# Edge tiles beside the first 7 of 8 groups in three joined stages of a graph network

## The chip, the cores and the metric

The kernel runs on one core of a Trainium2 chip. The metric is the device time of one execution in microseconds (us). Three runs of the kernel before took 3811.76, 3812.99 and 3815.6 us; the median is 3812.99.

## The reference

The input `x` has 10000 nodes of 512 features, and there are 5000 edges, sorted by target. Four graph layers follow each other, each as `x = layernorm(x + layer(x))`: a GIN layer, a SAGE layer with a batch norm, a layer of two graph attentions (GAT) and a product, and a GCN layer with a batch norm. Only the last two matter here:

```python
def gat_conv(x, src, dst, W, a_src, a_dst, bias):
    h = (x @ W).reshape(n, H, C)                       # H = 4, C = 256
    al_s = jnp.einsum('nhc,hc->nh', h, a_src)
    al_d = jnp.einsum('nhc,hc->nh', h, a_dst)
    e = jax.nn.leaky_relu(al_s[src] + al_d[dst], NEG_SLOPE)
    w = jnp.exp(e - segment_max(e, dst)[dst])
    alpha = w / segment_sum(w, dst)[dst]
    out = segment_sum(h[src] * alpha[:, :, None], dst)
    return out.reshape(n, H * C) + bias
...
h = relu(gat_conv(x, src, dst, W1, a_src1, a_dst1, b1))    # W1: 512 x 1024
h = relu(gat_conv(h, src, dst, W2, a_src2, a_dst2, b2))    # W2: 1024 x 1024
h @ Wfc + bfc                                              # Wfc: 1024 x 512
...
msgs = norm[:, None] * (x @ W.T)[row]                      # the GCN layer
out = segment_sum(msgs, col)
```

src and dst hold the edges and one loop from each node to itself.

## The kernel before, in words

The nodes are put in an order of the kernel's own and padded to 10240 rows, which makes 20 groups of 4 subtiles of 128 rows (S = 4). Nodes that are no edge's target stand first. The first 8 groups (`d.early`, E = 8) hold such nodes alone: their rows depend on no edge. The 5000 edges fill T = 40 tiles of 128. A float32 product is made of three float16 products (`split_product`, lines 350 to 352: low times high, high times low, high times high).

The program is a list of stages. At a stage's end all five engines meet, and none starts the next stage before. Inside a stage each engine has its own list, written out by hand, and they are held together by semaphores alone.

Three stages are joined: they work on the 8 edge-free groups and, beside them, on the edges' tiles, whose sums the stage behind needs for the other 12 groups.

- The middle stage, `gat_middle_early_stage`: the product with W2 for 8 groups. Each of 32 subtiles has three thirds of 344 columns, 24 matmuls each, so there are 96 slots, each one product. The edges' tiles are those of the first attention.
- The rows stage, `rows_product_early_stage`: the product with Wfc, 24 matmuls of 512 columns for each of 32 subtiles, so 32 slots. In a slot TensorE first turns two chunks of the next group (L3102), then makes the product. VectorE adds the product to the rows `x` (the residual, L3046, in float32), takes their moments (L1847, L1850) and, after slot 1 of the next group, applies the norm in `finish` (L1867). GpSimd makes the low halves (L3022), the norm's power (L1856, L1859) and starts the gathers. SyncE loads the rows to come (`load_rows`), `x` (`load_x`, L2987) and stores the results (`store`, L2992). The edges' tiles are those of the second attention.
- The GCN stage, `gcn_early_stage`: the product with the GCN's W, 12 matmuls for each of 32 pairs of group and quarter, so again 32 slots. Its edges' tiles are plain weighted sums (`RowEdges`).

`AttentionEdges` has T + 5 = 45 steps. Step e below 40 is tile e: TensorE multiplies the gathered rows by the mixing matrix `a_lhs` (L1700, eight passes), then sums the weights of the tile after (L1687) and turns the scores of the one after that (L1679). VectorE's step e makes the matrix of tile e + 1 (L1509 to L1521) and the maxima of tile e + 2. ScalarE copies the sums out (L1665), SyncE stores them with the first and the last row apart (L1450 to L1452). Steps 40 to 44 are the join of targets that lie in two tiles: VectorE waits until every tile is stored and spreads the last rows (step 40, L1546, L1547), TensorE turns them (step 41, L1714), VectorE and ScalarE weigh them (step 42), TensorE turns the weights (step 43, L1718) and VectorE copies them (L1586), TensorE sums the rows (step 44, L1723) and VectorE adds them (L1593), and SyncE stores (L1461). `RowEdges` has 41 steps: 40 tiles (L1827, two passes; copied out at L1811) and one join step, in which TensorE itself waits for all stores and sums the last rows (L1819); VectorE's part of it (`vector_end`, L1789, L1791) stands after its whole loop, and SyncE's store after that.

`shared_out` says which steps go behind which product. In all three stages each engine runs, for slot n, its part of the product and then its part of every step in `steps[n]`:

```python
steps = shared_out(edges.steps(), E * S)
...
for s in range(S):
    if g + 1 < E:
        turn(g + 1, (2 * s, 2 * s + 1))
    ...
    for e in steps[g * S + s]:
        edges.tensor_step(pe, e)
```

SyncE stores a tile one slot later than the others work on it (`waiting`).

Of the kernel before, what the change touches and what calls it, by code (L numbers as in the profile page):

```python
# [18 lines left out]
S = 4  # L19
# [12 lines left out]
THIRDS = 3  # L32
# [1794 lines left out]
        pe.matmul(self.total[t % 2][:], self.lhs[t % self.L], self.rows[w], start=True, stop=True).then_inc(self.summed.sem, 1)  # L1827


def shared_out(steps, slots):  # L1830

    return [range(n * steps // slots, (n + 1) * steps // slots) for n in range(slots)]
class Norm:


# [734 lines left out]
def gat_middle_early_stage(kn):  # L2570
# [4 lines left out]
    E = d.early  # L2575
    N = E * S
# [29 lines left out]
    wide_done = take("wide_done", THIRDS * N)  # L2606
    wide_stored = pair("wide_stored", 16 * 2 * E)
    edges = AttentionEdges(kn, mem, dram["h1"])
    steps = shared_out(edges.steps(), THIRDS * N)

    def sync(sp):
        def load_rows(j):
# [330 lines left out]
def rows_product_early_stage(kn):  # L2943
# [4 lines left out]
    E = d.early  # L2948
# [22 lines left out]
    rows_out = take("rows_out0", S * E)  # L2971
    stored = pair("stored", 16 * (E // 2))
    edges = AttentionEdges(kn, mem, dram["h2"])
    steps = shared_out(edges.steps(), E * S)

    def sync(sp):
        def load_rows(g):
# [406 lines left out]
def gcn_early_stage(kn, held):  # L3384
# [4 lines left out]
    E = d.early  # L3389
# [13 lines left out]
    seen = take("h_seen", 4 * E)  # L3403
    room = [held.rows[g][m] for g in range(E, E + 3) for m in range(4)]
    edges = RowEdges(kn, room, dram["x3"], (kn.src_by[:, :, 0], kn.src_dinv_neg), kn.dst_dinv, kn.rim_dinv)
    steps = shared_out(edges.steps(), 4 * E)

    def sync(sp):
        def load(g):
# [324 lines left out]
def graph_layers_kernel(nc, nodes, edges, io):  # L3734
# [16 lines left out]
    with ExitStack() as ctx:  # L3751
        kn = Kernel(nc, ctx, d, dram)
        tables = Tables(kn)
        with ExitStack() as mem:
            setup = setup_stage(kn, mem, tables)
            weights = plain_weights(kn, mem, list(range(W_SAGE_L + 1)), 3)
            sums = edge_sum_stage(kn, mem, dram["x"], None, None, None, tables)
            kn.add({
                "sync": in_turn(weights["sync"], setup["sync"], sums["sync"], setup["sync_late"]),
                "gpsimd": in_turn(setup["gpsimd"], sums["gpsimd"]),  # L3760
                "scalar": in_turn(setup["scalar"], weights["scalar"], sums["scalar"]),
                "vector": in_turn(setup["vector"], weights["vector"], sums["vector"]),
                "tensor": in_turn(setup["tensor"], sums["tensor"])})
        kn.add(gin_stage(kn))
        with ExitStack() as mem:
            kn.add(edge_product_stage(kn, mem))
        kn.add(sage_stage(kn))
        kn.add(norm_coefficients_stage(kn, V_SAGE_G, V_SAGE_BETA, 1.0 / UNSCALE))
        kn.add(batch_norm_stage(kn, "sage"))
        kn.add(gat_middle_early_stage(kn))  # L3770
        kn.add(gat_middle_stage(kn))
        kn.add(rows_product_early_stage(kn))
        kn.add(gat_stage(kn, 2))
        with ExitStack() as mem:
            held = Held(kn, mem)
            kn.add(gcn_early_stage(kn, held))
            kn.add(gcn_stage(kn, held))
            kn.add(norm_coefficients_stage(kn, V_GCN_G, V_GCN_BETA))
            kn.add(output_stage(kn, held))
        kn.run()  # L3780
# [60 lines left out]
```

How the kernel before makes its waits and increments, by code:

```python
        def program(eng, which):  # L310
            self.sig.raise_all(eng, ENGINES.index(which))
            eng.drain().then_inc(meet, 1)
            eng.wait_ge(meet, 5)
            for n, stage in enumerate(stages):
                if which in stage:
                    stage[which](eng)
                eng.drain().then_inc(meet, 1)
                eng.wait_ge(meet, 5 * (n + 2))
# [207 lines left out]
    def sync(sp):  # L526
        sp.dma_start(pairs[:], dram["edges"]).then_inc(pairs_in.sem, 16)
        sp.dma_start(dst_row, dram["dst"].partition_broadcast(P)).then_inc(dst_in.sem, 16)
        sp.dma_start(kn.vec[:], dram["vectors"]).then_inc(small_in.sem, 16)
        sp.dma_start(kn.gin_b2[:], dram["gin_b2"].partition_broadcast(P)).then_inc(small_in.sem, 16)
        sp.dma_start(kn.fc_b[:], dram["fc_b"].partition_broadcast(P)).then_inc(small_in.sem, 16)
        sp.wait_ge(blank_ready.sem, blank_ready.at(1))
        sp.dma_start(dram["sum"][d.none:d.none + 1, :], blank[0:1, 0:D]).then_inc(tables.zeroed.sem, 16)
        sp.dma_start(dram["sum_gat"][d.none:d.none + 1, 0:HC], blank[0:1, 0:HC]).then_inc(tables.zeroed.sem, 16)
        sp.dma_start(dram["sum_gat"][d.none:d.none + 1, HC:], kn.ones[0:1, 0:HEADS]).then_inc(tables.zeroed.sem, 16)
# [1 line left out]
    def sync_late(sp):  # L538
        sp.wait_ge(degrees.sem, degrees.at(2))
        sp.wait_ge(place_steps.sig.sem, place_steps.sig.at(9))
        sp.dma_start(dram["by_node"].rearrange("(p r) c -> p (r c)", p=P), kn.by_node[:].rearrange("p r c -> p (r c)"))\
```

## Time and profile before

| | us |
|---|---|
| three runs | 3811.76, 3812.99, 3815.6 |
| the profiled execution, its own time | 3817.86 |
| its span, from the first to the last instruction | 3816.0 |
| TensorE busy | 3332.8 (87% of the span) |
| VectorE busy | 1998.9 (52%) |
| ScalarE busy | 1430.8 (37%) |
| GpSimd busy | 1638.7 (43%) |
| products of the middle stage | 1645 to 2079 |
| products of the rows stage | 2650 to 2976 |
| products of the GCN stage | 3337 to 3467 |

Engines are called PE (TensorE matmul), PEld (its weight loads), DVE (VectorE), ACT (ScalarE), POOL (GpSimd) and SP (SyncE). A busy share is an average over stages with different limits, so each stage is read by itself. In a timeline a row gives the start and the length in us, and in brackets the idle time before it and what ended that. Matmuls overlap: a matmul's start to the next one's start is what it costs.

### The profile page before, as it was taken

Reading aid. Unit: us, or ns where it says so; the run is one execution under the profiler, and the core shown is the slowest. Engines: PE = TensorE matmul, PEld = TensorE weight load, DVE = VectorE, ACT = ScalarE, POOL = GpSimd, SP = SyncE. Lnnn points to the kernel's source line nnn. Section 1 sums busy time; section 2 is a strip of 40 time slices with the busy share of each in tenths; the row PEclk is TensorE's granted clock in tenths of the full one; section 3 lists DMA queues with packets and bytes.
Section 4 is the critical chain, followed back from the end, with each engine's and each line's share of the span. In section 5 each row is a group of like instructions: output and inputs, shape, how many; then the busy total and the mean of one; then the engine's idle time right before and its main releaser. Section 6 shows DMA issues by size and latency. Waiting matters only on the chain. (4 is left out here: it accounts for less than half of the span.)

```text
span 3816.0 us, 54506 instructions
## 1 busy us (share of the span) xinstructions
PE 3332.8 (87%) x18968; PEld 2029.2 (53%) x18968; DVE 1998.9 (52%) x3718; ACT 1430.8 (37%) x2551; POOL 1638.7 (43%) x1419
## 2 busy tenths in 40 slices
PE   4669998989988999979998899998989599897953
PEld 3224443445645766657775566665655355453543
DVE  7347776754545444244442643402766488433676
ACT  1323332443324444333332333323544244253366
POOL 3347775323547666322111432312544466322346
PEclk7789999989989999989999999998999799998975
DMA  2667774655659989698884989844775577366466
GB/s 82 202 174 197 201 196 122 222 163 182 213 193 252 284 270 274 198 233 224 223 217 139 259 210 207 199 109 157 223 240 183 214 258 259 138 214 172 144 216 225
DMA packets 601425, 771.73 MB, mean 202 GB/s; under 512 B 382934, under 2 KB 383190, under 8 KB 599200
## 3 DMA queue, kind: packets, MB, share of 16 engines
q1 hardware_dynamic: 525344, 535.62, 47.5%
q0 software_dynamic: 75904, 233.90, 21.4%
q8 instruction: 93, 1.52, 0.2%
q14 instruction: 84, 0.69, 0.1%
HBM read 420.55 MB, written 263.75 MB: 179 GB/s over the span
## 5 line engine op out<-in xcount | busy, mean ns | idle before, releaser
L351 PE MATMUL bank<-w_lo,t_r_hi 128*128 128x344 f16 (+1 forms) x2560 | 839.1, 328 | 0.0
L352 PE MATMUL bank<-w_hi,t_r_hi 128*128 128x344 f16 (+1 forms) x2560 | 838.8, 328 | 0.0
L350 PE MATMUL bank<-w_hi,w_lo 128*128 128x344 f16 (+1 forms) x2240 | 717.0, 320 | 47.2 <-DMA w_lo<-g_row_lo 31.3
L351 PE MATMUL bank<-w_lo,w_hi 128*128 128x344 f16 (+1 forms) x1280 | 420.3, 328 | 0.0
L352 PE MATMUL bank<-w_hi 128*128 128x344 f16 (+1 forms) x1280 | 420.0, 328 | 0.0
L350 PE MATMUL bank<-w_hi 128*128 128x344 f16 (+1 forms) x1216 | 396.8, 326 | 22.9 <-DMA w_hi<-t_row_lo 19.4
L352 PEld LDWEIGHTS bank<-w_hi,t_r_hi 128*128 128x128 f16 x2560 | 251.4, 98 | 169.6 <-issue 1.7
L351 PEld LDWEIGHTS bank<-w_lo,t_r_hi 128*128 128x128 f16 x2560 | 251.4, 98 | 160.9 <-issue 1.3
L350 PEld LDWEIGHTS bank<-w_hi,w_lo 128*128 128x128 f16 x2240 | 219.9, 98 | 178.9 <-issue 42.8
L1438 POOL DMA_INDIRECT a_own<-h,edge_tables x80 | 82.2, 1028 | 533.8 <-PE bank L1700 388.0
L350 PE MATMUL bank<-l_z_hi,w_lo 128*128 128x512 f16 x640 | 245.1, 383 | 1.4 <-DVE l_z_lo L3562 1.4
L2875 DVE SCALAR_TENSOR_TENSOR t_z<-w_lo,t_z 128x256 f32<-128x256 f32 x192 | 139.5, 784 | 203.2 <-DMA w_lo<-h 200.7
L351 PE MATMUL bank<-l_z_lo,w_hi 128*128 128x512 f16 x640 | 245.1, 383 | 0.0
L352 PE MATMUL bank<-l_z_hi,w_hi 128*128 128x512 f16 x640 | 244.9, 383 | 0.0
L2849 POOL TENSOR_TENSOR t_row_lo<-t_r,t_row_hi 128x1024 f16<-128x1024 f32 x48 | 105.7, 2203 | 281.9 <-ACT t_row_hi L2896 281.8
L2515 ACT ACTIVATE b_wide<-bank 128x344 f32<-128x344 f32 x240 | 109.0, 456 | 252.6 <-PE bank L352 251.3
L1700 PE MATMUL bank<-a_rows,a_lhs 128*128 128x256 f32 x640 | 158.0, 391 | 23.9 <-DVE a_lhs L1521 23.9
L350 PEld LDWEIGHTS bank<-w_hi 128*128 128x128 f16 x1216 | 119.8, 99 | 96.9 <-issue 21.4
L352 PEld LDWEIGHTS bank<-w_hi 128*128 128x128 f16 x1280 | 125.9, 98 | 85.1 <-issue 0.8
L351 PEld LDWEIGHTS bank<-w_lo,w_hi 128*128 128x128 f16 x1280 | 125.8, 98 | 84.0 <-issue 0.7
L1878 POOL DMA_INDIRECT t_z<-sum_gat,slot_i x96 | 99.9, 1040 | 116.9 <-SPq L317 91.2
L1700 PEld LDWEIGHTS bank<-a_rows,a_lhs 128*128 128x128 f32 x640 | 121.8, 195 | 47.7 <-DVE a_lhs L1521 28.8
(413 smaller groups left out, 6889.3 us busy)
## 6 DMA issues: line engine op xcount, KB each, us to landing
w_lo<-h SPq DMA_DIRECT2D x154, 512.0 KB, 6.3
h<-b_wide SPq DMA_DIRECT2D x80, 516.0 KB, 3.4
h<-w_hi SPq DMA_DIRECT2D x80, 516.0 KB, 2.9
sum_gat<-a_out SPq DMA_DIRECT2D x80, 514.0 KB
sum<-e_out SPq DMA_DIRECT2D x80, 256.0 KB
g_x<-in_x SPq DMA_DIRECT2D x20, 1024.0 KB, 5.4
x<-g_y SPq DMA_DIRECT2D x20, 1024.0 KB, 5.0
h<-l_h SPq DMA_DIRECT2D x20, 1024.0 KB, 6.1
```

Of the source, the lines that this page charges most:

```text
L350: pe.matmul(out, s_lo, m_hi, start=(k == 0), stop=False)
L351: pe.matmul(out, s_hi, m_lo, start=False, stop=False)
L352: mm = pe.matmul(out, s_hi, m_hi, start=False, stop=last)
L1438: pool.indirect_dma_start(self.own[w][:], None, self.logits_dram, bass.IndirectOffsetOnAxis(ap=kn.dst_logits_i[:, t:t + 1], axis=0), bound ...
L1700: ins = pe.matmul(self.total[h // 2][:, (h % 2) * C:(h % 2 + 1) * C], self.lhs[:, h, :], self.rows[w][:, LOGITS + h * C:LOGITS + (h + 1) * ...
L1878: pool.indirect_dma_start(out, None, sums, bass.IndirectOffsetOnAxis(ap=kn.slot_i[:, g * S + s:g * S + s + 1], axis=0), bounds_check=kn.d. ...
L2515: act.activation(wide[s][:, n * THIRD:(n + 1) * THIRD], mm[n], ACT.Copy, scale=UNSCALE)\
L2849: nc.gpsimd.tensor_tensor(row_lo[:, s, :], r_f[s % 2][:], row_hi[:, s, :], ALU.subtract)\
L2875: ins = v.scalar_tensor_tensor(out=z[u][:, s, cols], in0=hrow[:, s, cols], scalar=z[u][:, s, HC + h:HC + h + 1], in1=z[u][:, s, cols], op0 ...
```

## The change

`shared_out` takes a number of slots at the end that get no step. The steps are spread over the slots before them. In the middle stage 12 of 96 slots are left free, in the two others 4 of 32: in each, those of the last group. Every engine's list follows, since all of them read `steps`.

```diff
-def shared_out(steps, slots):
-
-    return [range(n * steps // slots, (n + 1) * steps // slots) for n in range(slots)]
+def shared_out(steps, slots, free):
+
+    used = slots - free
+    return [range(n * steps // used, (n + 1) * steps // used) if n < used else range(0) for n in range(slots)]
...
-    steps = shared_out(edges.steps(), THIRDS * N)
+    steps = shared_out(edges.steps(), THIRDS * N, THIRDS * S)
...
-    steps = shared_out(edges.steps(), E * S)
+    steps = shared_out(edges.steps(), E * S, S)
...
-    steps = shared_out(edges.steps(), 4 * E)
+    steps = shared_out(edges.steps(), 4 * E, 4)
```

## Rows read from the trace of the kernel before

**Rows 1.** Busy time in stretches: middle stage, its first group, rows stage, GCN stage.

```profile
core 0: us, PE busy (x) PEld busy (x) DVE busy (x) ACT busy (x) POOL busy (x), PEclk, DMA share, GB/s
1652.00:2083.00 431.00, 426.02 (x2837) 308.27 (x2835) 180.93 (x496) 146.43 (x316) 72.87 (x72) 1.00 0.79 203
1645.00:1699.00 54.00, 51.10 (x328) 36.44 (x329) 22.23 (x59) 17.68 (x37) 8.02 (x8) 0.97 1.08 231
2656.00:2977.00 321.00, 293.87 (x1523) 186.99 (x1521) 215.00 (x560) 148.67 (x302) 145.04 (x140) 0.97 0.65 203
3340.00:3467.00 127.00, 127.00 (x564) 64.45 (x563) 40.18 (x58) 74.40 (x134) 34.13 (x34) 1.00 0.61 194
```

**Rows 2.** TensorE's waits in the rows stage: total us, times, longest.

```profile
PE bank L1700 <- DVE a_lhs L1521: 23.9, 11, 6.2
...
PE bank L1714 <- DVE a_rows L1547: 2.2, 1, 2.2
```

**Rows 3.** Timeline of TensorE in the rows stage, slots 1 and 2.

```profile
2659.18 0.38 PE L350 MATMUL bank<-w_hi 128*128 128x512 f16 x1
...
2664.36 1.89 PE L1700 MATMUL bank<-a_rows,a_lhs 128*128 128x256 f32 x8
...
2666.69 1.04 PE L3102 MATMUL bank<-ident,w_lo 128*128 128x128 f32 x8
2667.57 0.38 PE L350 MATMUL bank<-w_hi 128*128 128x512 f16 x1
...
2676.19 1.99 PE L1700 MATMUL bank<-a_rows,a_lhs 128*128 128x256 f32 x8 [0.94 <-DVE a_lhs L1521]
...
2679.80 0.38 PE L350 MATMUL bank<-w_hi 128*128 128x512 f16 x1
```

**Rows 4.** Timeline of slot 24 in the rows stage, TensorE and VectorE.

```profile
2903.39 0.38 PE L350 MATMUL bank<-w_hi 128*128 128x512 f16 x1
...
2912.79 0.69 DVE L3046 SCALAR_TENSOR_TENSOR w_hi<-bank,w_hi 128x512 f32<-128x512 f32 x1 [5.03 <-DMA w_hi<-x_biased]
...
2915.79 3.78 PE L1700 MATMUL bank<-a_rows,a_lhs 128*128 128x256 f32 x8 [4.72 <-DVE a_lhs L1521]
...
2921.68 0.38 PE L350 MATMUL bank<-w_hi 128*128 128x512 f16 x1
```

**Rows 5.** Busy time in the stretch of slot 30, after the join's first wait.

```profile
2965.50:2968.80 3.30, 3.30 (x9) 1.22 (x8) 1.73 (x4) 0.28 (x1) 0.00 (x0) 0.50 0.22 78
```

**Rows 6.** Timeline of the end of the rows stage.

```profile
2978.53 3.10 PE L1723 MATMUL bank<-a_last,a_rows 40*40 40x256 f32 x8 [1.86 <-DVE a_rows L1586]
2978.63 1.01 POOL L1859 TENSOR_TENSOR n_power<-n_power,minus_half 128x4 f32<-128x4 f32 x1
...
2982.94 1.90 DVE L1867 TENSOR_SCALAR w_hi<-w_hi,n_moments,n_power 128x512 f32<-128x512 f32 x4
```

**Rows 7.** Timeline of the end of the GCN stage.

```profile
3468.20 0.69 DVE L3448 BATCH_NORM_STATS2 bn_stats<-w_lo 128x6 f32<-128x512 f32 x1 [2.75 <-ACT w_lo L3467]
...
3471.70 1.92 PE L1819 MATMUL bank<-w_lo,edge_tables 40*40 40x512 f32 x2 [3.40 <-DMA w_lo<-w_lo]
3473.74 0.68 DVE L1789 TENSOR_TENSOR w_lo<-bank,w_lo 40x512 f32<-40x512 f32 x1 [4.84 <-PE bank L1819]
```

**Rows 8.** The end of the middle stage, and how long its stores L2632 take.

```profile
2078.95 1.92 PE L1723 MATMUL bank<-a_last,a_rows 40*40 40x256 f32 x8
...
2079.60 0.32 SPq L2632 DMA_DIRECT2D h<-w_hi  x1
...
2084.88 1.04 ACT L2910 COPY t_r<-vec 128x1024 f32<-128x1024 f32 x1 [5.30 <-SPq L317]
...
DMA to landing us min/median/max: 2.6/3.5/5.6
```

**Rows 9.** Timeline in the rows stage, slot 19, VectorE and GpSimd.

```profile
2850.31 0.16 DVE L1471 TENSOR_TENSOR a_score<-a_rows,a_own 128x4 f32<-128x4 f32 x1
2850.38 2.82 DVE L1472 TENSOR_TENSOR a_score<-a_own 128x4 f32<-128x4 f32 x1
...
2850.91 2.27 POOL L3022 TENSOR_TENSOR w_hi<-t_r,t_r_hi 128x512 f16<-128x512 f32 x2
```

## The prediction

> **What bounds the kernel now.** I read first the table of stretches, one for each joined stage [rows 1]. In the middle stage (gat_middle_early_stage) TensorE is busy 426.0 of 431.0 us and in the GCN stage (gcn_early_stage) 127.0 of 127.0, at a granted clock of 1.00: TensorE's own work sets both. In the rows stage (rows_product_early_stage) it is busy 293.9 of 321.0 at 0.97: 27 us are waits. Next, who ends them [rows 2]: 23.9 us in 11 waits for `a_lhs`, the mixing matrix that VectorE makes for each tile of edges, and 2.2 us in the join. Then the timeline shows where the 11 stand. The reader should see that a slot (one product) with one tile costs nothing but its work, and a slot with a pair of tiles makes TensorE wait for the second matrix [rows 3]. Last, the three ends [rows 6 to 8]: what stands between the last product and the next stage.
>
> **What the change does to the order.** Nothing is computed less or more. 45, 45 and 41 steps are shared over 84, 28 and 28 slots instead of 96, 32 and 32. In the middle stage a tile comes every 1.87 slots instead of 2.13, never two in a slot. In the rows stage, by the formula n*45//28 against n*45//32, slots with two tiles go from 11 (slots 2, 4, 7, 9, 12, 14, 17, 19, 22, 24, 27) to 15 (1, 3, 4, 6, 8, 9, 11, 13, 14, 16, 18, 19, 21, 23, 24). Step 40 falls to slot 25, steps 41 and 42 to slot 26, 43 and 44 to slot 27; slots 28 to 31 are bare products. In the GCN stage tile 39 and the join step 40 both fall to slot 27.
>
> **The rows stage, pairs.** From product to product a slot with one tile takes 2667.57 - 2659.18 = 8.39 us: product 5.18, tile 2.33 (2666.69 - 2664.36), next group's turn 0.88. Slot 2, a pair, takes 2679.80 - 2667.57 = 12.23, so its second tile costs 3.84, of which 2.33 is work, 0.94 the wait and 0.57 the restart around it [rows 3]. That is 1.51 above the work, the cheapest case. Over the stage the waits are 23.9 in 11, the longest 6.2 [rows 2]; the second longest is the 4.72 of slot 24 [rows 4]. Both stand in the first slot of a group, where VectorE's residual waits for the rows of `x_biased`: the load lands late, at 2912.79 the residual starts, and TensorE goes on 3.0 us later. The other nine share 13.0, or 1.44 each, so an ordinary pair costs 1.44 + 0.57 = 2.0. A pair in a group's first slot costs its wait (mean 5.5), 0.57, and a stretch at half clock, in which `L1700` takes 3.78 instead of 1.99. Slot 24 took 2921.68 - 2903.39 = 18.29; less the 11.29 of a pair without its wait and less 4.72, that stretch costs 2.2 beside the restart. Taking 5.5 + 0.57 + 2.2, a late pair costs 8.2.
> After: first slots with a pair are 4, 8, 16 and 24. For group 1 (slot 4) x is loaded ahead, so slot 4 is ordinary as now; 8, 16 and 24 wait for x, where now 12 and 24 do. Ordinary pairs go from 9 to 12: +3 x 2.0 = +6.0. Late ones from 2 to 3: +8.2. Bounds: with 1.51 for each of the twelve, and 18 for the nine now, +0; with 3.0 each, +18. The late one costs nothing if x is in time, 10 if it waits the longest 6.2 and more.
>
> **The rows stage, join.** Now step 40 and 41 share slot 29 and TensorE waits 2.24 [rows 2] for the copies; the clock then falls to 0.50, the lower of its two levels, for 3.3 us of the next product [rows 5], which costs half of that, 1.7. Both go, since step 40 gets a slot of its own: -3.9. In its place steps 43 and 44 stand in slot 27 behind each other. TensorE turns the weights, waits 1.86 for VectorE, which first has to take in product 27, and multiplies [rows 6]. Now that stands behind the last product; afterwards four products queue behind it. The wait is 1.9, the work 0.2 + 1.92 (the same eight passes at full clock in the middle stage [rows 8]), and the half clock that makes them 3.10 here costs 1.2 and some 0.5 of the next product: +5.8.
> The end: finish(7), `L1867` at 2982.94, now waits for the join's sums; without them it could start when GpSimd has the power, at 2979.64 [rows 6]. That returns -3.3. x for group 7, which now arrives late, is loaded after store(5), over 15 us before its residual; it is off the path.
> Sum: 6.0 + 8.2 - 3.9 + 5.8 - 3.3 = **+12.8**.
>
> **The GCN stage.** Here pairs cost only their work: TensorE has no wait up to the end. But step 40 makes TensorE itself wait until tile 39's rows are stored: 3.40 us [rows 7]. Now nothing is queued behind it. Afterwards product 28 and the three after it are. The join's two passes took 1.92 at half clock, so 0.9 at full; tile 39's two have the same width, 0.9. The last product ends later by both, by the wait of 3.4 and by a stretch at half clock. After 2.24 us of waiting that cost 1.7, after 4.72 it cost 2.2 [rows 4, 5]; I take 2.1: +7.3. In return vector_end follows the last statistics at 3468.89 instead of 3473.74 [rows 7]: -4.8. vector_end itself, its store and its landing stay last on VectorE's list and are as exposed as before. Sum: **+2.5**. Bounds: +0.4 with no clock penalty, +4.
>
> **The middle stage.** The last product ends later by the join's eight passes, 1.92, which leave the end [rows 8]: TensorE's sum is the same. Then ScalarE copies out and SyncE issues the store of 516 KB, now at 2079.60, 0.65 after the product's end; afterwards at 2080.87 + 0.65 = 2081.5, landing 2.6 later at best [rows 8], at 2084.1, and the other engines meet after that. The next stage now starts at 2084.88. **0**, with bounds of -3 and +3: the first group's one wait (2.9 us idle of 54) stands beside a DMA share of 1.08 [rows 1], and the first tiles move into that stretch.
>
> **The sum.** 12.8 + 2.5 + 0 = +15.3 us. The profiled execution took 3817.86 (span 3816.0 and 1.9 around it), 4.9 above the median; I add the difference to the median: 3812.99 + 15.3 = **3828.3**.
>
> **A rule weighed.** A small VectorE operation took 2.82 us, its neighbour of the same shape 0.16, while GpSimd's two subtractions ran from 2850.91 to 2853.18 [rows 9]. The Trainium skill, "SBUF — State Buffer", section "Who interferes with whom", says that a VectorE instruction with two SBUF inputs and a GpSimd instruction that reads SBUF exclude each other for the whole instruction. By that rule, the trace agrees, pairs would be dearer the more of them there are beside the subtractions: the sum would be the +26 worked out for the first rival, against +15.3 by the waits as they stand.
>
> **The rivals.**
> *The port.* In the denser order every pair meets such a subtraction. The price seen is 2.82 - 0.16 = 2.7 [rows 9]; on all twelve ordinary pairs +32, on four of them +11: total +26. For it: two subtractions stand in every slot up to 27. Against it: eight of the nine ordinary waits seen share 13.0 us and need no such price. 0.08.
> *Waits by time, not by number.* The 23.9 us could be what late DMAs cost however the tiles are placed. Then pairs add 0, the rest is -3.9 + 5.8 - 3.3 + 2.5 = +1.1: about 3814, the same. For it: x and the gathers are late by their own latency. Against: slots with one tile show no such wait. 0.18.
> *Pairs free, slower becomes faster.* Without last-group edges VectorE could have the second matrix ready in time. With p for an ordinary pair and 8.2 for a late one, the sum is 12p + 24.6 - 18 - 16.4 + 1.1 = 12p - 8.7, so it ends below -7.6 only for p under 0.1. The smallest p seen is 1.51. If the late ones vanish as well (-24.6), p up to 2.1 would do: with p = 1.5 the sum is -15, 3798. Against it: the load of x waits in SyncE's queue behind the same stores as now. 0.06.
> *DMA binds the middle stage.* Its DMA share is 0.79 over the stage with the last group nearly idle [rows 1]; a tile rate 14% higher in seven groups could bring back the first group's 2.9 in each: +20, total +35. For it: 1.08 in the first group. Against: products there are asked for three subtiles ahead. 0.08.
> The forecast, pairs dearer by number and a join in the middle: 0.60.
>
> **Chances and range.** Within 0.2% is within 7.6 us, about what a measurement of this kernel can tell. Slower: 0.60 + 0.08 + 0.08 less a tenth for a forecast whose pairs lie at the low bound: 0.70. Same: 0.22. Faster: 0.08. Range: from 3815, where waits go by time, to 3843, where the port or DMA comes in; 3820 to 3838 for the forecast alone.
>
> **What would show it.** Right: in the rows stage waits for `a_lhs` in 15 places and some 33 to 36 us, no wait at `L1714`, `L1723` after a wait of about 1.9 and followed by products, group 7 with products 5.2 apart. In the GCN stage `L1819` after about 3.4, then products at a clock of 0.50, and `L1789` at once after the last statistics. In the middle stage the same length. Wrong: 11 to 13 us less than that in the waits for `a_lhs`, or new waits for `turned_in` in the middle stage.

## The result and the profile after

The changed kernel takes 3834.19 us (median of six runs, 3831.01 to 3836.63), the kernel before 3812.38 in six runs beside it (3806.51 to 3816.85). The ratio is 1.0057, with a 95% interval of 1.0047 to 1.0067: slower by 21.8 us, beyond the 0.2% that tell a change from none, and inside the range given, 3815 to 3843. The forecast was +15.3. A few executions of the kernels below, and of the kernel before beside them, took 3943 us and more in a slower state of the chip, and are left out of every median and ratio.

The profiled execution took 3831.01 with a span of 3829.1. Against the span of 3816.0 before that is +13.1 only: before's profiled execution lay 5.5 above its median, this one 3.2 below. So each stage is compared by itself. A stage's length here runs from the stage's first load in SyncE's timeline to that of the next stage:

| us | before | after | difference | forecast |
|---|---|---|---|---|
| middle stage | 460.0 | 458.2 | -1.9 | 0 |
| rows stage | 367.1 | 379.5 | +12.4 | +12.8 |
| GCN stage | 152.1 | 156.0 | +3.9 | +2.5 |
| sum | | | +14.4 | +15.3 |

What is left of the 13.1, -1.3, is scatter of stages that the change does not touch: over all kernels below, the part ahead of the middle stage took 1622 to 1636 us, the stage behind it 535 to 542.

First the table of stretches, which answers to [rows 1]: middle stage, its first group, rows stage, the end of the GCN stage; then two stretches at half clock, one around the end of the long wait of slot 8 of the rows stage and one behind the join.

```profile
core 0: us, PE busy (x) PEld busy (x) DVE busy (x) ACT busy (x) POOL busy (x), PEclk, DMA share, GB/s
1645.00:2076.00 431.00, 430.70 (x2865) 311.30 (x2863) 181.99 (x497) 147.83 (x318) 72.52 (x72) 1.00 0.75 201
1645.00:1699.00 54.00, 54.00 (x354) 39.26 (x353) 23.07 (x63) 19.20 (x41) 10.03 (x10) 0.99 0.89 231
2656.00:2986.00 330.00, 293.21 (x1504) 185.77 (x1503) 215.24 (x559) 149.48 (x302) 146.03 (x140) 0.96 0.61 195
3472.80:3479.50 6.70, 6.28 (x13) 1.81 (x14) 0.00 (x0) 0.00 (x0) 0.00 (x0) 0.50 0.01 3
2745.70:2752.40 6.70, 3.52 (x8) 2.87 (x9) 4.36 (x14) 0.83 (x2) 0.00 (x0) 0.50 0.31 90
2967.60:2970.90 3.30, 3.30 (x10) 0.91 (x8) 1.28 (x2) 0.00 (x0) 0.00 (x0) 0.50 0.00 0
```

In the rows stage TensorE works as long as before (293.2 against 293.9 us) and is idle for 37 us instead of 27. In the middle stage it is idle for 0.3 us of 431, and in the first group for none of the 2.9 us of [rows 1]. That is not the change's doing: kernels below that leave this stage as it was (rows alone, GCN alone) show TensorE busy for 431.00 us of the stretch 1652 to 2083 as well. The wait of [rows 1] was one execution's.

TensorE's waits in the rows stage, which answer to [rows 2]:

```profile
PE bank L1700 <- DVE a_lhs L1521: 33.3, 16, 6.4
PE bank L1723 <- DVE a_rows L1586: 3.0, 1, 3.0
```

33.3 us in 16 waits for the mixing matrix (slot 4 has two) instead of 23.9 in 11, no wait at `L1714`, and one of 3.0 in the middle of the stage at `L1723`. The timeline of slots 8 and 24, the first of their groups, TensorE, VectorE and SyncE:

```profile
2734.85 0.38 PE L350 MATMUL bank<-w_hi 128*128 128x512 f16 x1
...
2736.36 0.59 SPq L2988 DMA_DIRECT2D w_hi<-x_biased  x1
...
2745.88 0.69 DVE L3047 SCALAR_TENSOR_TENSOR w_hi<-bank,w_hi 128x512 f32<-128x512 f32 x1 [6.66 <-DMA w_hi<-x_biased]
...
2748.88 3.76 PE L1700 MATMUL bank<-a_rows,a_lhs 128*128 128x256 f32 x8 [6.36 <-DVE a_lhs L1521]
...
2753.97 0.38 PE L350 MATMUL bank<-w_hi 128*128 128x512 f16 x1
...
2930.93 0.38 PE L350 MATMUL bank<-w_hi 128*128 128x512 f16 x1
...
2937.74 0.69 DVE L3047 SCALAR_TENSOR_TENSOR w_hi<-bank,w_hi 128x512 f32<-128x512 f32 x1 [4.26 <-DMA w_hi<-x_biased]
...
2940.73 3.41 PE L1700 MATMUL bank<-a_rows,a_lhs 128*128 128x256 f32 x8 [2.62 <-DVE a_lhs L1521]
```

Slot 8 took 19.1 us (2753.97 - 2734.85), for the reason of [rows 4]: VectorE's residual waits 6.66 us for the rows of `x`, the second matrix stands behind it, and TensorE waits 6.36. Slot 16 is its twin (6.13, 19.3 us). In slot 24 the wait is 2.62.

The join in slot 27, which answers to [rows 6], GpSimd, VectorE, then TensorE:

```profile
2960.75 2.39 POOL L3023 TENSOR_TENSOR w_hi<-t_r,t_r_hi 128x512 f16<-128x512 f32 x2 [4.57 <-ACT t_r_hi L3075]
...
2960.98 1.12 DVE L1574 TENSOR_TENSOR a_rows<-a_rows,a_r 40x164 f32<-40x164 f32 x1
2962.02 1.14 DVE L1577 TENSOR_TENSOR a_rows<-a_r,a_r 40x4 f32<-40x4 f32 x1
...
2964.14 0.67 DVE L3047 SCALAR_TENSOR_TENSOR w_hi<-bank,w_hi 128x512 f32<-128x512 f32 x1
...
2965.78 0.28 DVE L1586 COPY a_rows<-bank 40x160 f32<-40x160 f32 x1
...
2962.77 0.32 PE L1718 MATMUL bank<-ident,a_rows 40*40 40x40 f32 x4
...
2966.12 2.29 PE L1723 MATMUL bank<-a_last,a_rows 40*40 40x256 f32 x8 [3.02 <-DVE a_rows L1586]
2968.34 0.61 PE L350 MATMUL bank<-w_hi 128*128 128x512 f16 x1
```

The same operations in the kernel before:

```profile
2974.47 0.32 DVE L1574 TENSOR_TENSOR a_rows<-a_rows,a_r 40x164 f32<-40x164 f32 x1
2974.72 0.15 DVE L1577 TENSOR_TENSOR a_rows<-a_r,a_r 40x4 f32<-40x4 f32 x1
...
2976.35 0.32 PE L1718 MATMUL bank<-ident,a_rows 40*40 40x40 f32 x4
2976.53 0.69 DVE L3046 SCALAR_TENSOR_TENSOR w_hi<-bank,w_hi 128x512 f32<-128x512 f32 x1 [0.57 <-PE bank L352]
```

And the end of the stage: the last group's norm starts when GpSimd has the power.

```profile
2992.71 1.01 POOL L1860 TENSOR_TENSOR n_power<-n_power,minus_half 128x4 f32<-128x4 f32 x1
...
2993.76 1.91 DVE L1868 TENSOR_SCALAR w_hi<-w_hi,n_moments,n_power 128x512 f32<-128x512 f32 x4 [1.40 <-POOL n_power L1860]
```

The end of the GCN stage, which answers to [rows 7]:

```profile
3473.22 1.93 PE L1819 MATMUL bank<-w_lo,edge_tables 40*40 40x512 f32 x2 [3.40 <-DMA w_lo<-w_lo]
3475.08 0.61 PE L350 MATMUL bank<-l_z_hi,w_lo 128*128 128x512 f16 x1
...
3478.90 0.63 PE L350 MATMUL bank<-l_z_hi,w_lo 128*128 128x512 f16 x1
3488.55 0.69 DVE L3449 BATCH_NORM_STATS2 bn_stats<-w_lo 128x6 f32<-128x512 f32 x1 [1.90 <-ACT w_lo L3468]
3489.28 0.68 DVE L1789 TENSOR_TENSOR w_lo<-bank,w_lo 40x512 f32<-40x512 f32 x1
```

The join's wait of 3.40 us is the same as before, with products queued behind it that run at a granted clock of 0.50 (the matmuls shown take 0.61 and 0.63 us, at full clock 0.38), up to 3479.5. `L1789` follows at once after the last statistics.

### The profile page after: what moved, and what is told of

Its sections match the earlier page's. It is cut to its first block and busy times, and to the rows that moved or that the text cites. A ratio compares the mean times of both kernels' runs of the same rounds, so it can differ in the third digit from the quotient of the medians.

```text
span 3829.1 us, 54506 instructions
## 1 busy us (share of the span) xinstructions
PE 3336.5 (87%) x18968; PEld 2029.5 (53%) x18968; DVE 2005.2 (52%) x3718; ACT 1431.0 (37%) x2551; POOL 1637.8 (43%) x1419
## 3 DMA queue, kind: packets, MB, share of 16 engines
q8 instruction: 93, 1.52, 0.2%
## 5 line engine op out<-in xcount | busy, mean ns | idle before, releaser
L1700 PE MATMUL bank<-a_rows,a_lhs 128*128 128x256 f32 x640 | 160.8, 396 | 33.3 <-DVE a_lhs L1521 33.3
```

The source lines that it names most:

```text
L1700: ins = pe.matmul(self.total[h // 2][:, (h % 2) * C:(h % 2 + 1) * C], self.lhs[:, h, :], self.rows[w][:, LOGITS + h * C:LOGITS + (h + 1) * ...
```

## The experiments

Four sets, each on one chip beside the kernel before. The ratio is to the kernel before with its 95% interval; lengths are of the profiled execution, measured as in the table above. Line numbers are those of the changed kernel.

**One stage at a time.** `free` stays in one stage and is 0 in the two others (of the three edits, those in the middle, the rows and the GCN stage, each kernel has two).

```
-    steps = shared_out(edges.steps(), THIRDS * N, THIRDS * S)
+    steps = shared_out(edges.steps(), THIRDS * N, 0)
-    steps = shared_out(edges.steps(), E * S, S)
+    steps = shared_out(edges.steps(), E * S, 0)
-    steps = shared_out(edges.steps(), 4 * E, 4)
+    steps = shared_out(edges.steps(), 4 * E, 0)
```

> The change in the middle stage alone; the two other stages share out their steps as before. Theory (pairs and joins cost, the middle stage has neither): the stage keeps its length of 458.9 us from its first load to the next stage's within 3 us (457.0 in the changed kernel), no wait of TensorE for turned_in, and the time lies within 0.1% of before. Rival (DMA binds the middle stage once its tiles are denser): waits of some 2.9 us in several groups, +10 us or more.

> The change in the rows stage alone. Theory (dearer pairs, a join in the middle): the stage takes 371.6 us as in the changed kernel instead of 359.0, 15 waits for a_lhs of some 32 us in total, and the time is 12 to 13 us above before. Rival (the loss comes about only together with the other stages, or by chance of one execution): less than 5 us.

> The change in the GCN stage alone. Theory (TensorE's own wait for the last tile's stores now stands ahead of four products, then half clock): the stage takes 150.5 us instead of 146.4, TensorE waits 3.4 us at the join's product and product 28 runs at a clock of 0.50, and the time is some 4 us above before. Rival (the saved end of 4.8 us pays for it): within 1 us of before.

The fourth is the changed kernel itself, unchanged, for the sum on the same chip.

> The changed kernel once more, to measure its difference from before a second time beside the three parts. The three stages of its one profile are 14.8 us longer in sum (-1.9, +12.7, +4.1), while the medians of six runs each are 21.8 us apart. Theory (the stages are the whole of it, the rest is scatter between runs): 14 to 22 us above before, and the sum of the three single parts within 4 us of it. Rival (something outside the three stages adds 7 us whenever all three are changed): 20 us or more here, with parts that sum to less than 16, and a stage behind one of the three that is longer each time.

| | ratio | middle | rows | GCN |
|---|---|---|---|---|
| middle alone | 1.0002 (0.9993 to 1.0010) | 458.4 | 366.1 | 151.8 |
| rows alone | 1.0036 (1.0023 to 1.0048) | 457.4 | 382.0 | 152.2 |
| GCN alone | 1.0015 (1.0006 to 1.0023) | 456.6 | 366.4 | 155.5 |
| all three | 1.0057 (1.0044 to 1.0070) | 459.0 | 378.1 | 154.9 |

The three parts add up: 0.0002 + 0.0036 + 0.0015 = 0.0053 against 0.0057. The middle stage costs nothing that can be measured, so the rival that DMA would bind it is false. Its whole stretch with the new order, in the kernel with the middle stage alone:

```profile
1654.00:2085.00 431.00, 431.00 (x2865) 311.43 (x2863) 181.50 (x497) 147.80 (x317) 72.71 (x72) 1.00 0.76 202
```

TensorE is never idle there. (Kernels that don't have the change in this stage show 457 us (rows alone, GCN alone) as well as 460 us (before) for it, so its -1.9 is no gain that can be told from scatter.)

**Where the rows stage's 12 us come from.** Four edits on the changed kernel. First, the rows of `x` are asked for one slot earlier, ahead of the gathers' loads:

```
+                if s == 0 and g >= 2:
+                    load_x(g)
                 if s == 0 and g + 2 < E:
                     load_rows(g + 2)
...
-                if s == 1 and g >= 2:
-                    load_x(g)
```

> The changed kernel with one edit in SyncE's list of the rows stage: load_x(g) stands in slot 0 of group g, ahead of the stores of the tile before, instead of slot 1 behind them. Which slots hold a pair stays. Theory (a pair in a group's first slot is dear only because x is late): the three waits of about 6 us (slots 8, 16 and 24) fall to 1 to 2 us, their half-clock stretches go, and the rows stage shrinks from about 379.5 us to 361 to 365; in all +3 to +7 us to before instead of +22. Rival (TensorE waits there for VectorE's own work or for the gathers, x merely being last): the stage stays above 374.

Measured: 1.0023 (1.0013 to 1.0033), rows stage 369.8 us against 379.5 and 378.1, so 8 to 10 shorter. Slots 8, 16 and 24 take 13.9, 14.9 and 11.3 us instead of 19.1, 19.3 and 13.9. The timeline of slot 8, SyncE, VectorE and TensorE:

```profile
2727.50 0.58 SPq L2988 DMA_DIRECT2D w_hi<-x_biased  x1
...
2739.98 0.69 DVE L3047 SCALAR_TENSOR_TENSOR w_hi<-bank,w_hi 128x512 f32<-128x512 f32 x1 [1.08 <-PE bank L352]
...
2744.82 1.99 PE L1700 MATMUL bank<-a_rows,a_lhs 128*128 128x256 f32 x8 [2.61 <-DVE a_lhs L1521]
```

The residual now waits for the product itself and no longer for `x`, but 2.61 us of the wait for the matrix are left. Neither expectation was met: 369.8 lies above the theory's 361 to 365 and below the rival's 374. The three slots gave back 12.3 us and the stage 9.7, since others grew: slot 14 took 15.0 us instead of 12.6, and slot 12, with a single tile, 10.4 instead of 8.5. Early `x` moves waits to another place. VectorE's waits for `x` are gone (24.2 us in the changed kernel), and those for the gathered rows rise from 29.9 to 38.8.

Nor is late `x` the largest part of what the change costs, for the kernel before has late pairs too. With `x` early in both (the kernel before with early `x` follows below) the ratios are 1.0023 and 0.9973, 0.5% apart, against 0.57% with `x` late in both.

Second, the same fifteen pairs, `x` late again, but none of them in a group's first slot:

```
+    pairs = (1, 2, 3, 5, 6, 7, 9, 11, 13, 14, 17, 18, 19, 21, 23)
...
+        k = 0 if n > 24 else 2 if n in pairs else 1
...
+    steps[25:28] = [range(40, 41), range(41, 43), range(43, 45)]
```

> The changed kernel with the same number of pairs in the rows stage, 15, and the same join steps, but none of the pairs in the first slot of a group (pairs in slots 1, 2, 3, 5, 6, 7, 9, 11, 13, 14, 17, 18, 19, 21, 23). x is loaded where it was. Theory: the place sets the price, so all 15 cost the 2 us of an ordinary one; stage 361 to 365 us. Rival A (late x costs its time wherever the pairs stand, since VectorE then runs behind): stage 372 or more, with waits of some 5 us in slots 9, 13 and 17. Rival B (waits by number alone): stage unchanged at 379.

Measured: 1.0033 (1.0021 to 1.0046), rows stage 374.9. The slots 8, 16 and 24 fall to 8.5, 8.4 and 7.8 us, as singles do, but two others, 6 and 14, rise. VectorE ahead of the second matrix of slot 6, then TensorE's two waits:

```profile
2727.17 1.24 DVE L1471 TENSOR_TENSOR a_score<-a_rows,a_own 128x4 f32<-128x4 f32 x1 [3.56 <-DMA a_rows<-h,edge_tables]
...
2731.19 1.91 DVE L1868 TENSOR_SCALAR w_hi<-w_hi,n_moments,n_power 128x512 f32<-128x512 f32 x4
2733.02 0.68 DVE L3054 SCALAR_TENSOR_TENSOR w_hi<-bank,w_hi 128x512 f32<-128x512 f32 x1
...
2736.02 2.80 PE L1700 MATMUL bank<-a_rows,a_lhs 128*128 128x256 f32 x8 [3.57 <-DVE a_lhs L1521]
...
2830.69 3.78 PE L1700 MATMUL bank<-a_rows,a_lhs 128*128 128x256 f32 x8 [3.44 <-DVE a_lhs L1521]
```

Slot 6 takes 16.4 us and slot 14 17.0, against 12.7 and 12.6 in the changed kernel. So the theory that a pair out of a first slot costs 2.0 wherever it stands fails. Rival A has the length right (372 or more), but not the place: slots 9, 13 and 17 wait 1.8, 1.7 and 2.1 us and not 5. The three late pairs cost 20.2 in the changed kernel; as ordinary ones at 2.1 they would have given back 14, and 4.6 arrived.

Slots 6 and 14 are the third of their groups, where VectorE runs `finish` (L1868, 1.91 us) ahead of the residual. The kept traces show when that is dear. In slot 6 `finish` starts 6.6 us after the product's start, in the changed kernel 4.2. VectorE is late because of the slot ahead, a pair too: it waited 3.56 us for the gathered rows, and the small operation behind took 1.24 us instead of 0.16 beside a subtraction of GpSimd. In slot 14 it was 2.02 us for the rows, then an operation of 0.17 us that took 2.50. In all kernels of this document the pairs in the third slots of groups 1 to 5 fall in two kinds: where `finish` starts at most 4.3 us after the product, the slot takes 12.2 to 13.0 us (29 slots), and where it starts 6.0 to 6.6 us after, 15.0 to 18.0 us (eight slots). A pair in the slot ahead does not do it alone: slot 18 here follows a pair, has its `finish` at 4.2 and takes 12.6.

Third, the rows stage's last two join steps in slots of their own, 43 in slot 27 and 44 in slot 28:

```
     steps = shared_out(edges.steps(), E * S, S)
+    steps[27:29] = [range(43, 44), range(44, 45)]
```

> The changed kernel with the last two join steps of the rows stage in slots of their own: step 43 in slot 27, step 44 in slot 28. Theory (TensorE waits there because VectorE has to take in product 27 before it copies the turned weights): no wait at the join's sums, no half clock behind them, stage 4 to 5 us shorter than the 379.5 of the changed kernel. Rival (the wait is that of the chain itself, or the sums cost their half clock anyway): less than 1.5 us.

Measured: 1.0040 (1.0027 to 1.0053), rows stage 377.3. The timeline of TensorE in slot 28:

```profile
2975.03 0.38 PE L350 MATMUL bank<-w_hi 128*128 128x512 f16 x1
...
2975.77 1.92 PE L1723 MATMUL bank<-a_last,a_rows 40*40 40x256 f32 x8
2977.62 0.39 PE L350 MATMUL bank<-w_hi 128*128 128x512 f16 x1
```

The join has no wait, and the next product goes on at full speed, as the theory has it. From product 27 to product 31 it takes 23.0 us instead of 27.7. The whole stage is only 2.2 shorter and not 4 to 5, since slot 24 took 16.3 us in this execution and 13.9 in the other: its wait is 3.84 instead of 2.62.

Fourth, the same in the GCN stage, tile 39 in slot 27 and the join in slot 30:

```
     steps = shared_out(edges.steps(), 4 * E, 4)
+    steps[27], steps[30] = range(39, 40), range(40, 41)
```

> The changed kernel with the GCN stage's join step in slot 30 instead of slot 27 beside tile 39, so that three products stand between the last tile and TensorE's wait for its stores. Theory: the wait of 3.4 us and the half clock behind it (3 us) go, vector_end follows the last statistics at once, and the stage takes 148 to 149.5 us, below the 152.1 of before. Rival (the products of the last group then wait for something else, or vector_end is held up): 151 or more.

Measured: 1.0042 (1.0029 to 1.0054), GCN stage 149.4 us instead of 156.0, and below the 152.1 of the kernel before. TensorE's timeline:

```profile
3475.76 0.38 PE L350 MATMUL bank<-l_z_hi,w_lo 128*128 128x512 f16 x1
3476.50 1.05 PE L1819 MATMUL bank<-w_lo,edge_tables 40*40 40x512 f32 x2
3477.48 0.39 PE L350 MATMUL bank<-l_z_hi,w_lo 128*128 128x512 f16 x1
```

Three products cover the way of the rows to memory and back. The 6.6 us are the wait of 3.4 and a half-clock stretch of 3.15.

**Number against time.** To part "pairs dearer by number" from "waits by time" once more, `x` early and twenty slots with two tiles each, none with one:

```
+    steps = [range(2 * n, 2 * n + 2) if n < 20 else range(0) for n in range(E * S)]
+    steps[25:28] = [range(40, 41), range(41, 43), range(43, 45)]
```

> The run with x early, but all 40 tiles of the rows stage in pairs, in slots 0 to 19, so 20 pairs instead of 15; join steps where they were. Theory (a price for each pair, 2.5 us over its work): 12 us more in slots 0 to 25 than the 284.2 of the run with x early, so 294 to 299. Rival (waits by time: VectorE, the gathers and the stores need so long whatever the slots): within 4 us of 284.

Measured: 1.0081 (1.0060 to 1.0102), rows stage 393.4 us, 23.6 above its twin with fifteen pairs (x early). Its waits:

```profile
PE bank L1700 <- DVE a_lhs L1521: 38.5, 23, 3.9
```

Five more pairs cost 25.3 us from product 0 to product 25 (309.5 against 284.2; the theory had 294 to 299, the rival 288 at most), some 5 each, more than twice the 2.0 that I had. Both are missed, and the rival by more. The work that no longer stands beside products 20 to 24 is no gain: all of it lies on the path wherever it stands. The dearest slots are 6, 10, 14 and 18, each the third of its group, with 16.3 to 18.0 us and a `finish` 6.3 to 6.6 us after the product. So the price goes by how late VectorE is, and the gathers, which time rules, are a part of that: VectorE's waits for gathered rows are 48.2 us here.

**A version that is faster.** What the runs had shown was put together: tiles in 28 slots, twelve pairs, none of them in a first slot, `x` early; the rows stage's join in slots 28 (step 40), 29 (41 and 42), 30 (43) and 31 (44); in the GCN stage tiles over 28 slots and the join in slot 30.

```
+    pairs = (2, 5, 7, 9, 11, 13, 15, 18, 19, 22, 23, 26)
...
+        k = 0 if n > 27 else 2 if n in pairs else 1
...
+    steps[28:] = [range(40, 41), range(41, 43), range(43, 44), range(44, 45)]
...
+    steps = shared_out(edges.T, 28) + [range(0), range(0), range(edges.T, edges.T + 1), range(0)]
```

> The kernel before with what the runs so far pay for. Rows stage: load_x in slot 0 as in the run with x early; 40 tiles over slots 0 to 27 with 12 pairs, none in a group's first slot; join steps 40 in slot 28, 41 and 42 in 29, 43 in 30, 44 in 31. GCN stage: tiles over 28 slots, join step in slot 30. Middle stage as before. Theory: the rows stage loses the join's 3.9 us, 3.3 at its end and the two late pairs' extra 12, and pays for one pair more: 348 to 353 us instead of 366.5; GCN stage 149.4 instead of 152.1; in all 16 to 21 us below before, a ratio of 0.9945 to 0.996. Rival (waits go by time: what is taken from one place comes back at another): above 0.998.

Beside it, the kernel before with `x` early alone, and the version just shown with `x` late:

> The kernel before with load_x of the rows stage in slot 0 alone, sharing of steps untouched. Theory: its two late pairs (slots 12 and 24, 19.5 and 18.3 us) become ordinary ones of 13 to 14, the stage goes from 366.5 to 354 to 358 us, the ratio is 0.997 to 0.9975. Rival (as with the changed kernel, where three slots gave 5.2, 4.4 and 2.6 us back but others grew): above 360.

> The better version without the early load of x. Theory: no pair stands where x is late, so little is lost by it: the rows stage takes 352 to 358 us, 4 us more than with x early, as moving the pairs left slots 6 and 14 at 16 to 17 us. Rival (late x costs wherever the pairs stand): 10 us or more above the version with x early.

| | ratio | rows | GCN |
|---|---|---|---|
| new version | 0.9968 (0.9957 to 0.9980) | 358.1 | 149.0 |
| before, x early | 0.9973 (0.9962 to 0.9984) | 364.2 | 151.8 |
| new version, x late | 0.9969 (0.9958 to 0.9980) | 355.0 | 148.8 |

The new version's waits in the rows stage:

```profile
PE bank L1700 <- DVE a_lhs L1521: 15.2, 11, 2.3
```

It is faster than the kernel before by 0.3% (medians 3808.95 against 3820.51), between the theory's 0.9945 to 0.996 and the rival's 0.998. The stages give 9.0 + 3.1 = 12.1 us of that. The rows stage missed the 348 to 353 expected: from product 0 to product 27 it is 3.3 us longer than before and from there to product 31 9.3 shorter. But it has 39 tiles ahead of product 27, where the kernel before has 37, and two tiles are 4.2 us of work. Without that the first part is 0.9 shorter and the second 5.1: no step of the join makes TensorE wait for more than half a us. The end gives 3.3. With `x` late it is as fast (355.0, where 4 us more than with `x` early were expected): once no pair stands in a group's first slot, TensorE doesn't wait for the late load, though VectorE still does, 26.9 us in all.

Early `x` costs something too. In the new version the singles in slots 8 and 12 take 10.9 and 10.5 us, with `x` late 8.5 and 8.4. VectorE waits there until a store of SyncE's has landed, a wait that it has nowhere in this stage with `x` late:

```profile
2743.86 0.69 DVE L1493 TENSOR_REDUCE a_out<-a_masked 128x4 f32<-128x512 f32 x1 [2.41 <-DMA a_last<-a_out]
```

The kernel before with early `x` is as fast by its ratio, some 10 us, but its profiled execution shows a rows stage only 2.9 us shorter (364.2, above the rival's 360). In it slots 12 and 24 took 16.7 and 12.8 us instead of 19.5 and 18.3, and slot 8, a single, 14.5 instead of 9.0. VectorE there:

```profile
2749.35 0.16 DVE L1471 TENSOR_TENSOR a_score<-a_rows,a_own 128x4 f32<-128x4 f32 x1 [7.96 <-DMA a_rows<-h,edge_tables]
```

So a single is not always free of waits, as the prediction has it. That execution was the slowest of its eleven (3824.57, median 3811.22), so where the other 7 us lie is not shown.

## Why the prediction held, step by step

The direction, the two stages that lose and the mechanisms were as forecast; the sizes of four terms were not. The terms, from product starts in the timelines of before and after:

| term of the sum | forecast | measured |
|---|---|---|
| ordinary pairs, 9 to 12 | +6.0 | +9.4 |
| late pairs, 2 to 3 | +8.2 | +3.8 |
| old join | -3.9 | -3.9 |
| new join in slot 27 | +5.8 | +6.9 |
| end | -3.3 | -3.3 |
| GCN stage | +2.5 | +3.9 |
| middle stage | 0 | -1.9 |

**Ordinary pairs.** The price of 2.0 was too low. The twelve slots sum to 158.4 us, 13.2 each; less 8.39 for a single and 2.33 for the tile's work, 2.48. Their waits are 33.3 less the 6.36, 6.13 and 2.62 of the late ones, 18.2, or 1.52 each, about the 1.44 forecast. With the restart of 0.57 that is 2.1. What I left out is half clock: in slots 13 and 21, after waits of 1.98, the granted clock is 0.50 for 3.3 us, 1.7 us each. The trace of the kernel before had such a stretch already, in slot 19, which took 15.8 us; the nine of before measure 20.4 together where I put 18. The twenty pairs show that the price is not one number: it depends on how late VectorE comes.

**Late pairs.** 8.2 was right for slots 8 and 16 (8.4 and 8.6). Slot 24 cost only 3.2 by the same subtraction (its tiles, 38 and 39, are the last and turn nothing ahead; with the 1.1 us of work that they lack it is 4.3): its residual started 6.8 us after the product (2937.74 against a start at 2930.93), where in [rows 4] it was 9.4, and the wait was 2.62 instead of the 5.5 taken. Why `x` came sooner there isn't shown; the same slot took 12.5 and 16.3 us in other runs with the same code ahead of it. So two errors, +3.4 and -4.4, nearly cancel. That is luck: the stage's +12.4 against +12.8 looks better than its terms (which add up to 12.9; 12.65 if the stage is taken from TensorE's first turn).

**The new join.** The wait is 3.02 instead of 1.86. In the kernel before VectorE took in the last product just before the turning of the weights ended; here it is still at step 42's work when product 27 is done, and its residual starts 1.05 us after the turning has ended, at 2964.14, not 0.14 before it. Two small operations are the reason: `L1574` and `L1577` took 1.12 and 1.14 us where they take 0.32 and 0.15 in the kernel before, beside GpSimd's two subtractions from 2960.75 to 2963.14. The Trainium skill, "SBUF — State Buffer", section "Who interferes with whom", says that such instructions of the two engines exclude each other for their whole length; the trace agrees: the two end at 2962.10 and 2963.16, and GpSimd's pair reaches its middle at 2961.95 and its end at 2963.14. The rival called the port (+26) didn't happen, but its mechanism did, here and in the dear slots of the experiments, and forecast and rival were not exclusive as I put them. It was at work before too: of VectorE's small operations on the edges in the rows stage, mostly 0.13 to 0.2 us long, 23 took over 0.4 in the kernel before (41.6 us together) and 24 after (42.1), the two of the join among them. What the change adds is only where they stand.

**The half clock in slot 27** came as forecast: 3.3 us at 0.50, and product 28 at 6.5 instead of 5.2.

**GCN stage.** Wait 3.40 as forecast, end as forecast. The term that was off is the clock: 0.96 on `L1819` and 2.2 on product 28, 3.15 together, where I took 2.1 by the stretches of 3.3 us in [rows 5]. The stretch here is 6.7 us long. Moving the join apart gave back 6.6, which is this 3.15 and the 3.4.

**Middle stage.** No new wait; timed alone it makes no difference, and its -1.9 is scatter.

**The rest.** The timed difference, 21.8 us, is above the 14.4 that the three stages show. The parts' ratios give 0.0053, 20 us, again above what their stages show (-1.6, +14.9 and +3.4, 16.7). Some 3 to 7 us are not placed: the part ahead of the middle stage scatters by 14 us from one kernel's profile to the next and the stage behind it by 7, and one profile of each kernel can't show them.

**Rivals.** Waits by time: false as a sum, 33.3 us instead of 23.9, and 25.3 us more for five more pairs; but its ground, late gathers, is what makes some pairs dear. Pairs free: false, the smallest extra is 1.5. DMA in the middle stage: false. The port: its sum false, its mechanism seen in both kernels.

## What to carry to other kernels

Where side work is dealt out over an engine's slots, look at the slot with two pieces, not at the mean: the second waits for what another engine must do in between, and a pair costs most where that engine is itself held up, by a late load or by gathers that the pair ahead has put off. A chain of small dependent steps through several engines belongs into slots of its own, with a piece of main work between each two: apart, the joins gave back 4.7 us in the rows stage and 6.6 in the GCN stage. Together with twelve pairs instead of fifteen and none in a first slot, and the middle stage as it was, that is -0.3% to the kernel before where the changed kernel is +0.6%. A load asked for earlier takes away one wait and can make others, as early `x` did. Count what a wait in mid-stream costs with the half clock behind it.

## What the runs showed of the hardware

A wait of TensorE is followed by half clock at one time and not at another, even in the same slot with a wait of the same length. Slot 13 of the rows stage in the changed kernel, then in the kernel with the change in the rows stage alone, each with the stretch around its second tile:

```profile
2806.94 3.66 PE L1700 MATMUL bank<-a_rows,a_lhs 128*128 128x256 f32 x8 [1.98 <-DVE a_lhs L1521]
2807.10:2810.50 3.40, 3.40 (x10) 2.69 (x11) 1.40 (x4) 0.21 (x1) 0.05 (x1) 0.50 0.68 183
...
2812.63 1.99 PE L1700 MATMUL bank<-a_rows,a_lhs 128*128 128x256 f32 x8 [1.98 <-DVE a_lhs L1521]
2812.60:2816.00 3.40, 3.33 (x20) 2.78 (x21) 1.75 (x5) 1.54 (x4) 0.85 (x2) 1.00 0.71 210
```

The slot takes 15.1 us in the first and 13.8 in the second. In the kernel with early `x` waits of 2.61 and 3.57 us were not followed by half clock either, and the eight passes behind them took 1.99 us. So the length of one wait does not tell its price: none, 1.7 us (slots 13 and 21) or 3.15 us (the GCN stage).
